# A Mamba-and-experts sandwich kernel: second gate and residual moved, first three convolution columns of all tiles made at once

## The reference, cut to what matters

```
# mixer (H = 8 heads, P = 64, G = 128, chunks of 128 tokens)
z, xbc, dt_raw = split(u @ in_proj_w.T)
xp   = pad(xbc, ((0,0), (3,0), (0,0)))
conv = conv_b + sum(xp[:, k:k+L, :] * conv_w[:, k] for k in range(4))
xbc  = silu(conv);  X, B, C = split(xbc)
Y    = (C B^T * decay * dt) X + (C * exp(cum)) Hprev + D_skip * X
y    = rmsnorm(Y * silu(z)) @ out_proj_w.T

# feed-forward
sim = q(x) . keys;  top-8 of both halves;  scores, indices = top-8 of their sums
w   = silu((x . down_embed[indices]) * softmax(scores))
out = sum(w * up_embed[indices]) + silu(x @ W_up.T) @ W_down.T
```

## Time and profile before

| | |
|---|---|
| median of three runs | 2841.09 us |
| the profiled execution | 2840.37 us |
| its span, first to last instruction | 2838.7 us |
| granted TensorE clock, mean | 0.972 |
| TensorE busy | 2684.0 us, 95% |
| VectorE busy | 2449.3 us, 86% |
| GpSimd busy | 2100.9 us, 74% |
| ScalarE busy | 1737.2 us, 61% |
| from one group to the next, middle of the run | 85.33 us |

### The profile page before, as it was taken

One profiled execution on the slowest core, in us unless ns is written; L12 is line 12 of the kernel. 1 busy time (PEld: TensorE's weight loads), 2 busy tenths in 40 slices (PEclk: granted clock), 3 DMA queues, 4 the chain that ended last, 5 costly groups with the idle time before them and its releaser, 6 DMA issues. The chain is left out here.

```text
span 2838.7 us, 50280 instructions
## 1 busy us (share of the span) xinstructions
PE 2684.0 (95%) x14720; PEld 2215.7 (78%) x14720; DVE 2449.3 (86%) x6310; ACT 1737.2 (61%) x3656; POOL 2100.9 (74%) x2689
## 2 busy tenths in 40 slices
PE   5899999999999999999999999999999999999985
PEld 4778887878887878887878887878887878887864
DVE  4588898998888998889898889988889988989985
ACT  4566666666666566666666666666666666666643
POOL 3377777877777877777877777877777877777866
PEclk9999999999999999999999999999999999999998
DMA  3000000000000000000000000000000000000000
GB/s 133 8 8 12 5 7 11 11 11 11 4 7 11 11 11 11 4 7 11 11 11 11 4 7 11 11 11 11 4 7 11 11 11 8 7 7 11 8 5 8
DMA packets 28182, 34.23 MB, mean 12 GB/s; under 512 B 2672, under 2 KB 27248, under 8 KB 27440
## 3 DMA queue, kind: packets, MB, share of 16 engines
q1 hardware_dynamic: 28144, 33.77, 3.8%
HBM read 25.37 MB, written 8.39 MB: 12 GB/s over the span
## 5 line engine op out<-in xcount | busy, mean ns | idle before, releaser
L1079 DVE SCALAR_TENSOR_TENSOR acc<-bank,cw,acc 128x253 f32<-128x253 f32 (+2 forms) x1920 | 773.5, 470 | 0.0
L1405 PE MATMUL bank<-hT,w_in 128*128 128x256 f32 x2560 | 606.3, 382 | 11.4 <-DVE acc L1079 10.8
L594 POOL TENSOR_TENSOR Em<-ee 128x1024 f32<-128x1024 f32 x256 | 578.8, 2280 | 11.3 <-issue 11.3
L1405 PEld LDWEIGHTS bank<-hT,w_in 128*128 128x128 f32 x2560 | 485.0, 192 | 118.2 <-issue 44.5
L1238 DVE SCALAR_TENSOR_TENSOR Em<-Em,p 128x1024 f32<-128x1024 f32 x256 | 407.1, 1590 | 0.0
L609 POOL TENSOR_TENSOR W<-W,Em 128x1024 f32<-128x1024 f32 x128 | 337.0, 2633 | 8.5 <-ACT Em L887 0.3
L755 ACT ACTIVATE acc<-bank,cb,cw 128x256 f32<-128x256 f32 x640 | 325.1, 561 | 0.0
L1247 DVE TENSOR_TENSOR Em<-Em,products 128x1024 f32<-128x1024 f32 x256 | 310.9, 1214 | 4.5
L887 ACT ACTIVATE Em<-Em,rden 128x1024 f32<-128x1024 f32 x256 | 292.0, 1142 | 33.9 <-DVE Em L1247 33.9
L1574 PE MATMUL products<-w_de,h2T 128*128 128x512 f32 x512 | 234.5, 601 | 17.7 <-DVE Em L1247 17.7
L736 ACT ACTIVATE xbcT<-acc 128x512 f32<-128x512 f32 x320 | 200.6, 627 | 74.1 <-DVE acc L1079 74.0
(11 more groups left out here) (196 smaller groups left out, 5578.9 us busy)
## 6 DMA issues: line engine op xcount, KB each, us to landing
x_in<-x_dram SPq DMA_DIRECT2D x32, 256.0 KB, 2.7
x_res<-x_dram SPq DMA_DIRECT2D x32, 256.0 KB, 2.7
out_dram<-f SPq DMA_DIRECT2D x32, 256.0 KB, 2.2
w_in<-in_wT_dram SPq DMA_DIRECT2D x1, 3080.0 KB, 12.0
w_up<-upT_dram SPq DMA_DIRECT2D x1, 1024.0 KB, 14.7
w_de<-down_eT_dram SPq DMA_DIRECT2D x1, 1024.0 KB, 16.7
w_down<-downT_dram SPq DMA_DIRECT2D x1, 1024.0 KB, 18.7
w_ue<-up_e_dram SPq DMA_DIRECT2D x1, 1024.0 KB, 20.8
```

Of the source, the lines that this page charges most:

```text
L594: nc.gpsimd.tensor_tensor(Em[:, k], bc(ee[:, k, 0:XD], 2, KEYS), bc(ee[:, k, XD:XD + KEYS], 1, XD), ALU.mult).then_inc(E_done.sem, 1)
L1079: ins = V.scalar_tensor_tensor(acc[:, r, a, ahead:], ps[:, a * TOK:(a + 1) * TOK - ahead], cw[:, t, k:k + 1], acc[:, r, a, ahead:], ALU.mu ...
L1405: last = mm(ring[j % 2][:, a * TOK:(a + 1) * TOK], w_in[:, k, at:at + P], hT[:, k, :], start=k == 0, stop=k == DK - 1)
```

## The change

- VectorE's instruction for the first three columns of a tile goes (20 a group). ScalarE's halo copy now takes the first four and the last four columns into `edges`; GpSimd makes the first three columns of all 20 tiles in six small instructions once a group (`mixer_head`), and ScalarE takes their silu in one (`silu_head`). The other taps all cover 253 columns.
- VectorE's third mask of chunk 0 stands behind the second gate and the state step. GpSimd's first table of chunk 1 waits for that gate (`y_done`); its second comes behind the root of y, and the sum of the first two heads comes behind `tail_root3` and `tail_root4`, which is now in the same turn.
- VectorE's residual stands ahead of the first convolution of the turn.
- `ffn_last` is a copy; the scaling by the denominators is done once for both chunks in `ffn_choose`, and the factor from the products is the scale of ScalarE's silu.
- TensorE's matmul that zeroes the bank `f0` (L1614) goes; the first real one starts the bank. The transposes of X of chunk 0 stand behind the transposes of W and the expert products. On ScalarE the copy of X moves behind `ffn_WT(f, 1)`, and `ffn_norm` behind the second gate's square.

```diff
+            def mixer_head(g):
+                pool.wait_ge(halo_summed.sem, halo_summed.at(g))
+                pool.wait_ge(halo_taken.sem, halo_taken.at(g, PAIRS - 1))
...
+                nc.gpsimd.tensor_tensor(head[:], head[:], halo_sum[:], ALU.add).then_inc(own_pool, own.one())
+                pool.wait_ge(own_pool, own.n)
+                nc.gpsimd.tensor_tensor(head[:, :, 1:3], head[:, :, 1:3], head_b[:], ALU.add)\
+                    .then_inc(own_pool, own.one())
+                pool.wait_ge(own_pool, own.n)
+                nc.gpsimd.tensor_tensor(head[:, :, 2:3], head[:, :, 2:3], head_a[:], ALU.add)\
+                    .then_inc(head_summed.sem, 1)
...
+            def weigh(e, c, *heads, gate=None):
+
+                if gate is not None:
+                    pool.wait_ge(y_done.sem, y_done.at(gate, CH - 1))
...
-                if b:
-                    tail_root4(e)
...
                 if a:
                     mixer_cum(g)
                     mixer_parts(g)
+                    mixer_head(g)
...
                 if a:
                     mixer_scale(g, 1)
+                    mixer_decay(g, 1)
                 if c:
                     ffn_root(f)
-                if a:
-                    mixer_decay(g, 1)
-                if b:
-                    weigh(e, 1, 0, 1)
+                if b:
+                    weigh(e, 1, 0, gate=g)
                 if a:
                     mixer_root_y(g)
                 if b:
+                    weigh(e, 1, 1)
+                if a:
+                    tail_root3(g)
+                    tail_root4(g)
+                if b:
                     collect(e, 0, 1)
-                if a:
-                    tail_root3(g)
-                if b:
                     weigh(e, 1, 2, 3)
                 pool.wait_ge(own_pool, own.n)
...
+            def silu_head(g):
+                act.wait_ge(head_summed.sem, head_summed.at(g))
+                nc.scalar.activation(xbcT[:, :, 0:TAPS - 1], head[:], ACT.Silu).then_inc(head_done.sem, 1)
...
-                nc.scalar.activation(halo[:, 2 * j:2 * j + 2, :],
-                                     ps[:].rearrange("p (a t) -> p a t", a=2)[:, :, TOK - TAPS + 1:], ACT.Copy)\
-                    .then_inc(halo_taken.sem, 1)
+                nc.scalar.activation(edges[:, :, 2 * j:2 * j + 2, :],
+                                     ps[:].rearrange("p (a b c) -> p b a c", a=2, c=TAPS)[:, 0::TOK // TAPS - 1],
+                                     ACT.Copy).then_inc(halo_taken.sem, 1)
...
-                    nc.scalar.activation(cls[:], clz[:, c], ACT.Silu, accum_out=clsum[:, c:c + 1])\
+                    nc.scalar.activation(cls[:], clz[:, c], ACT.Silu, scale=last_a[:, 0:1],
+                                         accum_out=clsum[:, c:c + 1])\
...
                     ffn_up(e, 3)
                 if a:
                     silu(g, PAIRS - 2)
+                    silu_head(g)
                     silu(g, PAIRS - 1)
+                if c:
+                    ffn_WT(f, 1)
+                if a:
                     mixer_move(g, 0)
-                if c:
-                    ffn_WT(f, 1)
                 if b:
                     ffn_exp(e)
...
                     mixer_yT(g, 0)
-                if c:
-                    ffn_norm(f)
                 if b:
                     ffn_experts(e, 0, 1)
                 if a:
                     mixer_yT(g, 1)
                     mixer_square(g, 1)
+                if c:
+                    ffn_norm(f)
                 if b:
                     ffn_experts(e, 0, 2)
                     tail_keep(e)
...
-                if j == 0:
-                    dve.wait_ge(halo_summed.sem, halo_summed.at(g))
-                for a in range(2):
-                    t = 2 * j + a
-                    V.scalar_tensor_tensor(acc[:, r, a, 0:TAPS - 1], ps[:, a * TOK:a * TOK + TAPS - 1],
-                                           cw[:, t, TAPS - 1:TAPS], halo_sum[:, t, :], ALU.mult, ALU.add)\
-                        .then_inc(own_dve, own.one())
                 before = [0, 0]
                 for k in range(TAPS - 1):
-                    ahead = TAPS - 1 - k
                     for a in range(2):
                         t = 2 * j + a
                         if k:
                             dve.wait_ge(own_dve, before[a])
-                        ins = V.scalar_tensor_tensor(acc[:, r, a, ahead:], ps[:, a * TOK:(a + 1) * TOK - ahead],
-                                                     cw[:, t, k:k + 1], acc[:, r, a, ahead:], ALU.mult, ALU.add)
+                        ins = V.scalar_tensor_tensor(acc[:, r, a, TAPS - 1:],
+                                                     ps[:, a * TOK + k:(a + 1) * TOK - TAPS + 1 + k],
+                                                     cw[:, t, k:k + 1], acc[:, r, a, TAPS - 1:], ALU.mult, ALU.add)
...
+                dve.wait_ge(rden_done.sem, rden_done.at(e))
+                dve.wait_ge(own_dve, own.n)
+                V.tensor_tensor(masked, masked, bc(rden[:].rearrange("p c h -> p (c h)"), 2, NC), ALU.mult)\
+                    .then_inc(clz_done.sem, 1)
 
             def ffn_last(e, c):
 
                 dve.wait_ge(A_ps.sem, A_ps.at(e, c))
-                dve.wait_ge(rden_done.sem, rden_done.at(e))
-                V.tensor_copy(last_a[:], fA[:, EXPERTS - 1:]).then_inc(own_dve, own.one())
-                dve.wait_ge(own_dve, own.n)
-                V.scalar_tensor_tensor(clz[:, c], clz[:, c], last_a[:, 0:1], bc(rden[:, c], 2, NC),
-                                       ALU.mult, ALU.mult).then_inc(clz_done.sem, 1)
+                if c or later(e):
+                    dve.wait_ge(cls_done.sem, cls_done.at(e, c - 1))
+                V.tensor_copy(last_a[:], fA[:, EXPERTS - 1:]).then_inc(last_done.sem, 1)
...
-                conv(0)
                 if b:
                     tail_residual(e)
-                conv(1)
+                conv(0, 1)
                 if c:
                     ffn_last(f, 1)
                     ffn_mask(f, 1, 0)
...
                     mixer_state(g, 1)
                 if b:
                     ffn_times(e, 0, 1)
-                    ffn_mask(e, 0, 2)
                 if a:
                     mixer_gate(g, 1)
                     mixer_step(g, 1)
                 if b:
+                    ffn_mask(e, 0, 2)
                     ffn_times(e, 0, 2)
                 if c:
                     ffn_store(f)
...
                 if c == 0:
+                    pe.wait_ge(head_done.sem, head_done.at(g))
                     pe.wait_ge(conv_done.sem, conv_done.at(g, TILES - 3))
...
-                    mm(f0[:], zero_b[:], mask_b[:].rearrange("p h t -> p (h t)"), start=True, stop=False)
                 for i in range(FT):
                     last = mm(f0[:, c * D:(c + 1) * D], hid[:, i, c * P:(c + 1) * P], w_down[:, i, :],
-                              start=False, stop=False)
+                              start=c == 0 and i == 0, stop=False)
...
+                if c:
+                    ffn_WT(f, 1, None)
+                if b:
+                    ffn_A(e, 0)
                 if a:
                     mixer_X(g, 0)
-                if c:
-                    ffn_WT(f, 1, None)
-                if b:
-                    ffn_A(e, 0)
-                if a:
                     mixer_rows(g, 0, f)
```

42 lines of the change are left out of this document (27 added, 15 removed).

## The result

The changed kernel takes **2936.6 us** (median of 4 runs, 2934.3 to 2937.0) against 2841.3 (2840.7 to 2841.6) of the kernel before in the same session: a ratio of 1.033, with a 95% interval of 1.032 to 1.035. It is slower, inside the range and 28 us above the predicted 2909. Its profiled span is 2935.1 us.

What follows compares the result with a forecast made beforehand. TensorE was held by its wait for VectorE's second gate and the slow clock behind. +0.8 + 1.6 - 0.2 + 0.2 = +2.4 us a group, +72 over 30 edges, -4 at the ends: 2909 us; own range 2871 to 2945, 8-in-10 range down to 2800.

Steps and rivals of the forecast that it cites:

- The forecast case: At group edges, a new TensorE wait ahead of pair 2 with slow clock behind it: 2909 us, chance 0.56.
- The gate and the blocking: VectorE's gate multiply falls to 0.67 us; GpSimd's tables then block the mask by 1.05 and the store by 1.5.
- The residual's place: Ahead of convolution 0, VectorE's residual now waits 1.21 us behind `tail_sum` for GpSimd's root.
- Pair 2 +0.8: On TensorE, a new wait of some 4.5 us for convolution 0 starts pair 2 0.8 us later than before.
- 17.9 us of the chain: VectorE's chain up to convolution 0; the blocks-gone rival needed 2.4 us of it to fall away.
- The clock behind the new wait: TensorE's matmuls run at the slow clock behind the wait at pair 2: +1.6 us a group.
- 1.60 or twice that: Slow-clock loss behind TensorE's new wait if the clock falls; the other bound was none, and 1.6 was taken.
- Zeroing matmul and transposes of X, -0.2 and +0.2: On TensorE, the dropped matmul saves 0.2 us a group; B's transposes wait 0.2 (0 to 1) for the later decays.
- Sum: All terms for one group: +0.8 + 1.6 - 0.2 + 0.2 = +2.4 us.
- blocks gone: Rival: VectorE's mask and store meet no GpSimd table, the chain loses 2.55 us: 2784 to 2832 us, chance 0.23.
- Slower, but the clock holds: Rival: pair 2 comes 0.8 us later a group without slow clock: 2861 us, chance 0.10.
- At no cost: Small instructions, silu, edge copy and scaling add nothing; losing GpSimd's cover would delay the transposes of X about 2 us.

Runs made afterwards that it cites:

- the table moved late: The changed kernel with GpSimd's second weight table of chunk 1 put behind the two roots of the residual: 2871.7 us, ratio 1.011.
- the kernel with work in the wait: The changed kernel with four useless 128x512 matmuls in TensorE's stream ahead of pair 2: 2876.5 us, ratio 1.013.
- residual back: The changed kernel with VectorE's residual back between the first two convolutions, all else as changed: 2802.9 us, ratio 0.987.
- the residual alone: The kernel before with one edit, the residual ahead of both first convolutions: 2880.3 us, ratio 1.015.
- gate alone: The kernel before with VectorE's third mask behind second gate and step, GpSimd's chunk 1 tables released by the gate, state scaling ahead of f's root: 2815.9 us, ratio 0.992.
- heads and residual: The changed kernel without the gate's move: mask ahead of the second gate again, no wait for it on GpSimd; residual still first: 2928.2 us, ratio 1.031.
- heads alone: The changed kernel without its two moves: residual between the convolutions, second gate behind the mask, no wait for it on GpSimd: 2827.2 us, ratio 0.996.

## Why the prediction was right, and where its size was off

The forecast case came true, and nearly all of its mechanism. Step by step, from the end of L1522 (L1551 after, 1502.73), the ends in us:

| step | predicted | measured |
|---|---|---|
| gate done | +1.6 | +1.5 |
| mask, blocked by the released table | +4.8 | +4.6 |
| product | +6.0 | +5.8 |
| store, blocked by the second table | +8.2 | +7.8 |
| last mask and product | +10.6 | +10.3 |
| `tail_sum` | +12.5 | +12.1 |
| root waited for | +13.7 | +13.6 |
| convolution 0 done, pair 2 starts | +18.0 | +18.0 |

- **The gate and the blocking.** Right: 0.69 for the multiply, mask and store at 2.08 each, no wait left at the transposes. That it is the table that holds the store is shown by the table moved late: the store falls to 0.68 as a whole, and pair 2 comes 1.4 earlier.
- **The residual's place.** Right as the cause: one line undone gives 2802.9. The wait for the root was 1.51, not 1.21: the root itself ends 1.22 behind `tail_sum` (1514.87 to 1516.09), and another 0.29 go by before VectorE starts, which the prediction left out. Smaller steps ahead of it, the store above all, made up for that.
- **Pair 2 +0.8.** Measured +0.81. That it fits to a hundredth is luck in part, as the errors of 0.3 to 0.4 us in the steps cancel. (The prediction's "17.9 us of the chain" is 18.0 by its own steps.)
- **The clock behind the new wait.** This is the term that was mis-sized. I took 1.6, the loss behind 2.12 us of idle, and 2.28 were measured, by the kernel with work in the wait. The text named "1.60 or twice that" as the upper bound; the truth lies between, as low stretches of 7.0 us and of 3.5 us take turns (63.30 us behind pair 2 in one group of three, 64.1 to 64.3 in the others). Against the 61.61 at full clock a short stretch costs 1.69, near the 1.6, and a long one 2.47 to 2.67. What the prediction had not foreseen is that two groups of three would have a long one.
- **Zeroing matmul and transposes of X, -0.2 and +0.2.** At full clock the part behind pair 2 is 0.33 longer (61.61 less 61.28). Laid side by side, the two timelines give -0.21 for the zeroing matmul, as predicted, +0.44 at the decays and +0.10 on pair 2 itself, the first matmuls behind a wait. The wait for the decays is 0.22 us, as expected, but a wait costs more than its idle time (the rows below): the halves of L1498 start 0.82 us apart, where without a wait four such transposes take 0.45 to the next start (1504.35 to 1504.80). That is 0.37 for an idle time of 0.22.

```profile
1483.44 0.60 PE L1498 MATMUL bank<-ident,xbcT 128*128 128x128 f32 x4
1484.26 0.65 PE L1498 MATMUL bank<-ident,xbcT 128*128 128x128 f32 x4 [0.22 <-ACT Ldec L815]
```

- **Sum.** 0.81 + 2.28 + 0.33 = 3.42 a group against 2.4; the 1.0 over, times 30, less somewhat larger gains at the ends, are the 28 us.
- **The rivals.** The time of "blocks gone" (2784 to 2832) was reached by six kernels here, all with at least one block in place: it is enough that the residual no longer stands in front. With the residual in front and the store's block alone gone the time is 2871.7; no run takes away both blocks there, so that this rival's own case stays untried. "Slower, but the clock holds" (2861) would be the kernel with work in the wait (2876.5): that rival was priced 15 us too low, and did not happen.
- **At no cost.** GpSimd's heads make TensorE wait nowhere in a middle group of the change as it stands. With the residual back and the transposes of X moved back too, TensorE waits 2.40 us for them; I had named about 2 us, if their cover on GpSimd went, and had not seen that the transposes' place is what keeps it away.

## What to carry to other kernels

A wait that you remove does not vanish with its length: ask where the engine runs into next, and on what work its slow clock then falls. Here it cost 2.28 us a group behind the wait that ends last. A low stretch ahead of such a wait looks covered and may not be: with the residual alone, the engine that TensorE waited for had itself waited for the slow matmuls. Parts of a change should be tried alone and in pairs; two parts that gained 24 and 13 us lost 8 to 48 once the third, the residual in front, was there. And a move that looks like a pure cost (the later transposes of X) may be what another part of the change stands on.

## What I had not expected of the hardware

- The granted clock after waits of different kinds. With single waits of 0.99 and 0.42 us (residual back) or 0.96, 0.83 and 0.52 us (gate alone) a steady group shows no low clock at all. With waits of 1.01 and 2.25 us in one group (heads and residual) there is a low stretch of 3.75 us behind each. But with the heads alone the same wait of 1.01 us at the gate is followed by a low stretch in two of five groups in a row and by none in the other three, and with the table late a wait of 3.14 us is followed by none in one of three (pair 2 at 1225.80, against 1312 and 1398). Behind 3.97 us it is 3.5 or 7.0 us long, in a pattern of three groups: the long ones set in while TensorE still waits (1519.25, with pair 2 at 1520.74), the short ones 1.4 us after it has resumed (1434.00, with pair 2 at 1432.58). So the length of a wait does not decide it, and the rows do not settle what does.
- Behind the filler matmuls, with 0.54 us idle, the clock stayed at 1.00: adding 3.6 us of useless work to TensorE made the program 60 us shorter.
- A wait on TensorE costs its idle time and 0.1 to 0.2 us more: 0.37 for 0.22 at the decays; and in the changed kernel the products take 7.67 us to the start of pair 2 (1513.07 to 1520.74), 4.15 more than the 3.52 of before (1465.08 to 1468.60), for an idle time of 3.97.
